# A four-layer decoder: the norm behind the 32-head attention made batch by batch, the first batch's inside the attention's loop

## The reference

```
qkv = x @ w_qkv                      # 32 heads of 32
attn = softmax(q k^T * 32 ** -0.5)   # over the 256 rows of the batch
out = (attn @ v) @ w_out + b_out
mu, var = mean(out), mean((out - mu) ** 2)            # over the 128 columns
out = (out - mu) / sqrt(var + 1e-6) * ln_gamma + ln_beta
x = layernorm(x + out)                                # eps 1e-5
```

## Time and profile before

| | |
|---|---|
| median of three runs | 1298.23 us (1296.92 to 1298.74) |
| the profiled execution | 1299.21 us, span 1297.5 us |
| TensorE busy, matmul | 1159.9 us, 89%, 10601 instructions |
| VectorE busy | 910.8 us, 70%, 2412 |
| ScalarE busy | 688.2 us, 53%, 1307 |
| GpSimd busy | 234.1 us, 18%, 335 |
| granted TensorE clock | 0.963 of full speed |

### The profile page before, as it was taken

The page is one execution under the profiler, slowest core; times in us unless marked ns, Lnnn a source line. Parts: engine busy times, 40 slices in busy tenths (PEclk is TensorE's granted clock), DMA queues, the critical chain, the costliest instruction groups (busy, mean ns, idle before and its releaser), DMA issues. The chain is left out here.

```text
span 1297.5 us, 27470 instructions
## 1 busy us (share of the span) xinstructions
PE 1159.9 (89%) x10601; PEld 788.4 (61%) x10601; DVE 910.8 (70%) x2412; ACT 688.2 (53%) x1307; POOL 234.1 (18%) x335
## 2 busy tenths in 40 slices
PE   7789999999999999999889899797768898799975
PEld 4457767777777777676556575465445565456542
DVE  5472573646689859988888689957785866756376
ACT  2254464544564655455657546575426755377534
POOL 4320131203110120022201023011120112301122
PEclk8899999999999999999999999999969999899997
DMA  7002101111112101110000000000000000000000
GB/s 289 20 2 65 50 17 48 35 58 42 50 34 74 50 25 50 34 49 1 2 9 10 2 26 1 1 2 1 2 1 2 2 2 3 1 2 2 2 1 33
DMA packets 23288, 35.59 MB, mean 27 GB/s; under 512 B 4584, under 2 KB 12920, under 8 KB 22904
## 3 DMA queue, kind: packets, MB, share of 16 engines
q1 hardware_dynamic: 23160, 33.83, 8.3%
HBM read 32.77 MB, written 1.05 MB: 26 GB/s over the span
## 5 line engine op out<-in xcount | busy, mean ns | idle before, releaser
L2252 DVE TENSOR_REDUCE arena<-banks 128x4 f32<-128x1024 f32 x128 | 150.5, 1217 | 69.4 <-PE banks L2078 68.7
L1366 PEld LDWEIGHTS banks<-WE,arena 128*128 128x128 f32 x1536 | 180.2, 192 | 24.5 <-issue 23.6
L1366 PE MATMUL banks<-WE,arena 128*128 128x128 f32 x1536 | 182.6, 276 | 0.0
L1410 ACT ACTIVATE arena<-banks,BC 128x512 f32<-128x512 f32 x192 | 128.3, 691 | 94.3 <-PE banks L1350 94.1
L1350 PE MATMUL banks<-XT,WE 128*128 128x512 f32 x384 | 177.3, 597 | 0.5 <-ACT arena L1842 0.3
L2232 ACT ACTIVATE arena<-banks 128x1024 f32<-128x1024 f32 x128 | 124.1, 1022 | 63.2 <-PE banks L2103 63.2
L1450 DVE SCALAR_TENSOR_TENSOR R<-banks,arena,R 128x128 f32<-128x128 f32 x256 | 71.8, 343 | 103.2 <-PE banks L1366 102.6
L2333 POOL TENSOR_TENSOR arena<-arena 128x256 f32<-128x256 f32 x56 | 43.4, 774 | 379.8 <-ACT arena L2214 379.8
L615 ACT COPY arena<-banks 128x512 f32<-128x512 f32 x100 | 57.1, 587 | 99.7 <-PE banks L610 40.4
L1350 PEld LDWEIGHTS banks<-XT,WE 128*128 128x128 f32 x384 | 68.2, 190 | 65.7 <-issue 62.8
L1912 DVE TENSOR_TENSOR arena<-arena 128x512 f32<-128x512 f32 x144 | 100.8, 700 | 4.0
(11 more groups left out here) (333 smaller groups left out, 2117.0 us busy)
## 6 DMA issues: line engine op xcount, KB each, us to landing
WE<-in_weights SPq DMA_DIRECT2D x64, 256.0 KB, 2.9
WE<-in_weights SPq DMA_DIRECT2D x64, 128.0 KB, 2.2
WS<-in_weights SPq DMA_DIRECT2D x1, 2368.0 KB, 14.5
RW<-in_rows SPq DMA_DIRECT2D x1, 1032.0 KB
XALL<-in_x SPq DMA_DIRECT2D x4, 256.0 KB, 10.9
out_dram<-arena SPq DMA_DIRECT2D x4, 256.0 KB, 2.3
WS<-in_weights SPq DMA_DIRECT2D x1, 900.0 KB, 9.2
WS<-in_weights SPq DMA_DIRECT2D x1, 645.0 KB, 9.3
```

Of the source, the lines that this page charges most:

```text
L1366: ins = PE.matmul(v[:, tile(t)], self.HT[:, e % 2, j, tile(t)], self.W[:, (8 * i + e) % RING, 1, j], start=j == 0, stop=j == self.J - 1)
L1410: A.activation(self.HT[:, e % 2, j], psum.view(f"{self.L}.h{i}.{e}.{j}"), ACT.Relu, bias=bcol(self.p + "_b1", e * self.J + j))\
L2252: V.tensor_reduce(big.mx[:, 2 * pair:2 * pair + 2], v, AX.X, ALU.max, negate=True).then_inc(dve.read(f"big.m{i}.{n}.{pair}"), 1)
```

## The change

Nothing changes in what is computed. The attention's norm, the addition and the statistics of the next norm are made for two tiles at a time. For the first batch VectorE makes statistics, variance and scaling in round 13, behind the maxima of that round, and the addition and the next statistics in round 16, behind `invert(1)`. GpSimd raises the first batch's two variances to -0.5 ahead of its addition of round 14. At the end stand only the second batch's two tiles; the variance of the end norm, GpSimd's work for it and ScalarE's stay whole. `TURNS` and `FILLERS` are as before.

```
+        def half_of(i, b):
+            return slice(4 * i + 2 * b, 4 * i + 2 * b + 2)
+        def half_stats(dve, i, b):
+            dve.eng.wait_ge(*dve.own())
+            for t in (2 * b, 2 * b + 1):
+                V.bn_stats(st[:, 4 * i + t, :], R[:, i, t, :]).then_inc(dve.step(), 1)
+            dve.eng.wait_ge(*dve.own())
+            for t in (2 * b, 2 * b + 1):
+                V.bn_aggr(mv[:, 4 * i + t, :], st[:, 4 * i + t, :]).then_inc(dve.step(), 1)
+            dve.eng.wait_ge(*dve.own())
...
@@ end_sum_dve
-            norm_stats(dve, i, R[:, i], L, EPS)
+            if L == "big":
+                half_stats(dve, i, 1)
+                V.tensor_scalar(var[:, tiles_of(i)], mv[:, tiles_of(i), 1], EPS, None, ALU.add)\
+                    .then_inc(dve.flag(L + ".var"), 1)
+            else:
+                norm_stats(dve, i, R[:, i], L, EPS)
@@ big_dve
+            def norm(b):
+                half_stats(dve, i, b)
+                V.tensor_scalar(var[:, half_of(i, b)], mv[:, half_of(i, b), 1], 1e-6, None, ALU.add)\
+                    .then_inc(dve.flag("bign.var"), 1)
+                for t in (2 * b, 2 * b + 1):
+                    V.scalar_tensor_tensor(R[:, i, t], R[:, i, t], mv[:, 4 * i + t, 0:1], row("L3_attn_ln_gamma"),
+                                           ALU.subtract, ALU.mult).then_inc(dve.step(), 1)
+            def add_norm(b):
+                dve.eng.wait_ge(sig("big.xb"), i + 1)
+                dve.eng.wait_ge(sig("bign.rstd"), CB * i + b + 1)
+                dve.eng.wait_ge(*dve.own())
+                for t in (2 * b, 2 * b + 1):
+                    k = 4 * i + t
+                    V.scalar_tensor_tensor(R[:, i, t], R[:, i, t], rstd[:, k:k + 1], XB[:, slot(i), t],
+                                           ALU.mult, ALU.add).then_inc(dve.step(), 1)
...
                 if n == 12:
                     bias(0)
+                if n == 13:
+                    norm(0)
+                if n == 16:
+                    add_norm(0)
+                    half_stats(dve, i, 0)
                 yield
             divide(1, range(4))
             yield
             bias(1)
-            r = R[:, i]
-            norm_stats(dve, i, r, "bign", 1e-6)
-            scale_rows(dve, i, r, "L3_attn_ln_gamma")
+            norm(1)
             yield
-            dve.eng.wait_ge(sig("big.xb"), i + 1)
-            dve.eng.wait_ge(sig("bign.rstd"), i + 1)
-            dve.eng.wait_ge(*dve.own())
-            for t in range(4):
...
+            add_norm(1)
             yield from end_slots_dve(dve, "big", i)
@@ big_pool
+            def rstd_half(b):
+                pool.eng.wait_ge(sig("bign.var"), CB * i + b + 1)
+                G.tensor_tensor(rstd[:, half_of(i, b)], var[:, half_of(i, b)], minus_half[:, 0:2], ALU.pow)\
+                    .then_inc(pool.flag("bign.rstd"), 1)
...
             for n in range(GROUPS):
+                if n == 14:
+                    rstd_half(0)
                 if n % 8:
...
-            norm_rstd(pool, i, "bign")
+            rstd_half(1)
```

More of the change, by code:

```diff
@@ L528, in norm_rstd @@
             G.tensor_tensor(rstd[:, tiles_of(i)], var[:, tiles_of(i)], minus_half[:, 0:4], ALU.pow)\
-                .then_inc(pool.flag(name + ".rstd") if name in ("bign", "last") else pool.step(), 1)
+                .then_inc(pool.flag(name + ".rstd") if name == "last" else pool.step(), 1)
         def norm_shift(pool, i, name):
@@ L2311, in big_dve @@
             bias(1)
-            r = R[:, i]
-            norm_stats(dve, i, r, "bign", 1e-6)
-            scale_rows(dve, i, r, "L3_attn_ln_gamma")
+            norm(1)
             yield
-            dve.eng.wait_ge(sig("big.xb"), i + 1)
-            dve.eng.wait_ge(sig("bign.rstd"), i + 1)
-            dve.eng.wait_ge(*dve.own())
-            for t in range(4):
-                k = 4 * i + t
-                V.scalar_tensor_tensor(r[:, t], r[:, t], rstd[:, k:k + 1], XB[:, slot(i), t], ALU.mult, ALU.add)\
-                    .then_inc(dve.step(), 1)
+            add_norm(1)
             yield from end_slots_dve(dve, "big", i)
```

## The result

The changed kernel took 1306.49 us, the median of six runs (1301.45 to 1309.0), against 1298.22 for the kernel before on the same chip; the ratio is 1.0056, 95% interval 1.004 to 1.0072. The forecast, 1298.4 with 1294.5 to 1302.5, missed it. The profiled execution was the shortest of the six: 1301.45 us, a span of 1299.7. In the six, the longer times go with the lower mean granted clock: 0.964 and 0.965 at 1301.45 and 1303.37, 0.958 to 0.961 at 1306.3 to 1309.0.

The account below looks back on a forecast made before the run. No stage was taken as bound by one engine throughout (TensorE busy 89%, VectorE 70%). Chunk terms 0.7 + 0.95 - 0.8 - 0.7 = +0.15 us gave 1299.4 on the profiled run, forecast 1298.4 us, no change; 80% range 1294.5 to 1302.5.

Parts of the forecast that it names:

- Inserted 1.45 and 1.41: VectorE time, in us, that the work added to rounds 13 and 16 of a chunk was to take.
- 0.89 and 1.23: Round 16 of chunks 2 and 3: us of the inserted 1.41 still paid after VectorE's idle 0.52 and 0.18.
- Removed 1.91: End of each chunk's attention: us the chain was to lose; 2.16 where the power is not waited for (chunk 0).
- The power of two columns: GpSimd's power for two variances: about 0.8 us, 0.28 less than for four, hidden ahead of round 14's addition.
- Chunk 2: Net -0.8 us: round 13 free, 0.89 paid in round 16, TensorE able to use at most 1.71 - 0.89.
- its cover in round 13: Chunk 2: 1.54 us before the product needing the maxima's bank starts, against 1.45 inserted; without it 1.45 is paid.
- Chunk 1: Both insertions paid in full, 2.86 us, less 1.91 removed at the end: +0.95 us.
- The forecast's own sign of being wrong: Chunk 3: the prediction would be wrong if output(1) took more than 4 us.
- falls back to VectorE's pace: Chunk 0: TensorE loses waits as the end gives back 2.16 of the inserted 1.45 and 1.41 us: +0.7.
- The bound named beside it, 1.45: Chunk 0: if TensorE is the slower engine instead, it keeps at most round 13's 1.45 us.
- chunk 3's -0.7: Round 13 free, +1.23 us in round 16, 1.91 removed at the end: -0.7 us.
- The clock falls: Rival, 27%: longer TensorE waits bring half clock, up to +1.86 us on chunk 3's output(1); 1301.0, or 1302.8 us.

Follow-up runs that it names:

- e9: The changed kernel again, nothing altered, for one more profile: 1304.1 us.
- e1: The changed kernel again, nothing altered, on a second chip: 1310.52 us, ratio 1.0091 to the kernel before.
- e2: Changed kernel with only the round-13 part; first batch's addition and next statistics back at the end: 1304.59 us, ratio 1.0053 to the kernel before.
- e3: Changed kernel with the first batch's addition and statistics behind the second batch's division instead of in round 16: 1301.27 us, ratio 1.0026 to the kernel before.
- e5: The change in chunks 0 and 1 only, chunks 2 and 3 as before: 1302.72 us, ratio 1.0028 to the kernel before.
- e4: Changed kernel plus matmuls without a use ahead of output(1), 18 in chunk 1, 12 in chunk 3: 1301.24 us, ratio 1.002 to the kernel before.
- e15: The change in chunk 3 only, as it stands (rounds 13 and 16): 1298.76 us, ratio 1.0015 to the kernel before.
- e16: The change in chunk 3 only, with the addition in round 15: 1297.49 us, ratio 0.9993 to the kernel before.
- e13: The kernel before again, nothing changed, for a second profile: 1297.65 us.
- e14: The kernel before once more, nothing changed, for another profile: 1297.06 us.
- e10: The changed kernel again, nothing altered, for a further profile: 1307.55 us.
- e6: The change in chunks 2 and 3 only: 1300.63 us, ratio 1.0005 to the kernel before.

## Why the prediction was wrong

**The sizes were nearly right.** Inserted 1.45 and 1.41: VectorE's shift grew by 1.54 and 1.67 in chunk 0, 1.54 and 1.68 in chunk 1 (e9). In round 16 of chunks 2 and 3, where 0.89 and 1.23 were to be left behind VectorE's idle time, it grew by 1.06 and 1.41. Removed 1.91: 1.87 in chunks 1, 2 and 3. The power of two columns took 0.70 to 0.74 us where 0.8 was taken, but 1.15 in chunk 0's round 14, and ended before its addition. Chunk 2 came out at -0.7 for -0.8, its cover in round 13 held. Chunk 1 came out at +1.6 for +0.95, from profiles between -0.2 and +3.4, so this term is neither borne out nor refuted. The forecast's own sign of being wrong, output(1) of chunk 3 over 4 us, showed in three of the change's four profiles.

**Chunk 0 is the first failed step**, that TensorE "falls back to VectorE's pace", which made +0.7. At 783 VectorE stood 0.69 later than before, as summed; at 824 it was 1.55 later. TensorE did not fall back: it was 1.6 us late behind round 13 and 2.8 behind round 16, gave back about 1.1, its whole wait of 0.83 ahead of the transposes among it, and had no more waits to lose; now VectorE waited for it. From the profile after, TensorE and VectorE:

```profile
785.00 0.41 PE L596 MATMUL banks<-ident,XALL 128*128 128x128 f32 x2
...
786.54 2.36 DVE L1265 TENSOR_REDUCE arena<-banks 128x16 f32<-128x1024 f32 x2 [0.23 <-PE banks L1056]
```

The bound named beside it, 1.45, was about the value. Where two low stretches came in a row behind the longer wait (e1, e2, e3, e5), it was 2.0 to 2.5.

**The second, and the larger, is the treatment of the clock as a rival that happens or not**, outside the sum: chunk 3's -0.7 came out at +2.5. The rival "The clock falls" had place and price: output(1) of chunk 3 at 1.2 GHz, "up to +1.86". It came in three of the change's four profiles, at +2.8: at the low clock almost throughout the product takes 6.6 us and not the 5.67 of the earlier trace rows, which had a part at full clock. In the same three a second low stretch followed at 1256, inside the cross-attention. In all profiles of this study the product was slow in four of six with a wait of 3.3 us or more and in one of twelve with 2.1 us or less. Against three of four, the chance of 27% was low, and the price stood for chunk 3's product and one more slow stretch only. Chunk 1's output(1) took 5.53 to 6.64 us in the change's four profiles and 5.34 to 5.67 in the three of before, and 1.2 us of the loss lie in other places, where low stretches came or went without a cause that I can name. That the low clock is dear is shown best by e4; that the longer wait brings it is borne out by the profiles but not by e15 and e16, whose times do not differ clear of noise.

**The profile of before as base.** Behind 590 us its execution took 2.0 us longer than e13 and 4.1 longer than e14, with 9 and 10 us more of low stretches. I took its waits and products for those of the kernel; in e13 the wait ahead of chunk 1's output(1) was 3.71 us, not 2.86.

**Open.** Why the other runs of the change lie 2 to 6 us above its four profiles, on the average; a place for this is not shown. Their granted clocks give an estimate. The 98 runs of the kernel before in e1 to e16 lie near one line, 0.9 us longer for each 0.001 less of mean granted clock. At the same clock the change's runs lie above that line by 2.8 us on the first chip and 4.2 in e1; the other 4 and 6 us go with their lower mean clock, 0.961 and 0.959 against 0.965. That is a correlation and does not say which causes which. Open too is what decides, of two executions with the same wait, which gets the low clock (e1 and e15 against e9, e10, e6).

## What to carry over

Work that leaves a chain is best put where the engine's next instruction waits for someone else, with room on both sides: in chunks 2 and 3 the same 1.4 us gained nothing in round 16 (ratio 1.0005) and made a faster kernel in round 15 (0.9966). An insertion ahead of an engine that waits can be paid twice, once as delay and once as the chance that TensorE's next product runs at half clock (6.6 us for 3.8 in chunk 3, in three of four profiles); price both before moving anything. Where a wait can't be removed, matmuls without a use in it are the other way: they gave back 9.3 us of 12.4 (e4), as much as moving the addition out of round 16 did (e3).

## What was not expected of the hardware

The same kernel spreads by 10 us on one chip (1303.86 to 1313.78 in e1), the kernel before by 5 to 11. Low stretches come and go between executions of one kernel, and where one falls on a chain everything behind it shifts, here by 0.8 us (e2, chunk 0) to 2.8 (output(1) of chunk 3). The power on GpSimd took 0.70 to 0.74 us alone and 1.15 while VectorE ran maxima and minima of 128x512 beside it (750.03 in the profile after); the one of VectorE's that began at 749.52 took 1.10 us, its neighbours 0.68.
